# Building the retention masks on chip and reordering the first sequence of a decoder layer

## The chip, the core and the metric

The kernel runs on one NeuronCore of a Trainium2 chip. The metric is the device time of one execution in microseconds. A core has five engines with instruction queues of their own, each run in order: TensorE (PE), VectorE (DVE), ScalarE (ACT), GpSimd (POOL) and SyncE (SP), which here only issues transfers. They meet through semaphores.

## The reference

A post-norm decoder layer over 4 sequences of 256 tokens, width 256:

```
x = layernorm(x + retention(x))            # 16 heads, decay mask
x = layernorm(x + ssm(ctx_1024, gate=x))   # 256 channels x 16 states
x = layernorm(x + moe_ffn(x))              # 896 wide, LoRA experts, top 2 of 8
```

The part on masks, from the retention:

```
expn = jnp.maximum(diff, 0).astype(x.dtype)
dmask = jnp.where(diff >= 0, gamma[:, None, None] ** expn, 0.0)
scores = jnp.einsum('bhnd,bhmd->bhnm', q, k) * dmask
ret = jnp.einsum('bhnm,bhmv->bhnv', scores, v)
```

The retention output is normalised per head, times silu(x @ wg + bg), and projected with wo. The state space part projects the context, convolves it over 4 tokens, applies silu (u), makes a low-rank projection (dbl: step size, B and C rows), step sizes delta = softplus(...), and then state = state * exp(delta * A) + delta * u * B, y = sum of state * C, over 256 tokens.

## The kernel before

The four sequences form a pipeline written out by hand. `first(0)` on each engine computes retention and state space part of sequence 0; `stage(b, fb)` then interleaves those of sequence b with the feed-forward of fb = b - 1; the last stage has the feed-forward of sequence 3 alone. Every engine's order is the order of the calls in its block.

The state recurrence is cut into 16 units of 2 states x 256 tokens x 128 channels (`UNITS`). In `first`, a unit i needs `decays(i)` on ACT (L723, two exponentials), `drive(i)` on PE (L1186, four transposes of columns that ACT's `drive_columns` made, L874), `first_scan(i)` on DVE (L1794), `first_times_c(i)` on POOL (L630) and `add_states(i)` on PE (L1251, four transposes added into the bank acc). The ring has 4 tiles, `decay` has 2 and `drives` 3, so unit i waits for i - 4, i - 2 and i - 3.

Retention runs in chunks of 128 tokens. `scores(r)` (PE, L1322) for r = 0 to 3 fills the two gen banks, `decayed` (DVE, L1741) multiplies them by `dmask`, `values(r)` (PE, L1340) sums into ret. `token_keys` and `chunk_state` make the state that the first chunk hands to the second. `qdec` (128 x 2 x 128) holds the powers for the second chunk's queries, which POOL applies in `decayed_queries` (L611).

The masks: DVE doubles a row of powers of gamma for 16 heads seven times (L1618), SP stores it to DRAM with 16 copies, fetches it back skewed, 16 rows at a time, in eight transfers into `dmask` (L433), and twice into `qdec` (L437). SP issues the fetch of the first feed-forward weight W1 (L457) after these. The weights W1, W3, B1, B3 are split into a high part (a cast) and a low part (a subtraction), blocks of 128 x 448: `split_high`, `split_low`. In `first`, W1's four casts stand on DVE ahead of the first scan, W3's in the loop, the subtractions on POOL.

All matrix products of the first sequence's inputs (context IN, Q, DBL, DT, K, V, key transposes KN, GATE, KV) rotate through the two gen banks in the order `FIRST`. Six products of later sequences (`spare`) follow from unit 7 on, when the feed-forward banks are still idle. `conv` (DVE) needs xpad and cv from ACT's `conv_input`; u feeds `low_rank`, then `step_size` on PE, `softplus` on ACT, and `step_small`, `step_sum` on DVE, whose product with u is du; PE's `flip_inputs` (L1178) transposes du.

## Time and profile before

| | us |
|---|---|
| median of 3 runs | 425.17 |
| lowest, highest | 423.29, 426.05 |
| the profiled execution | 419.82 |
| its span | 418.1 |
| mean granted TensorE clock, share of full | 0.986 |

Busy over the span: PE 373.9 us (89%), weight load 320.6 (77%), DVE 298.5 (71%), POOL 214.9 (51%), ACT 188.8 (45%). These are means over the whole; the page also cuts the span into 40 slices with a tenths digit for each engine. In the timeline a row is a merged run of equal instructions: start, duration, engine and line, output and inputs by the program's names, count, and in brackets how long the engine had been idle before and what released it. An f32 product counts two matmul instructions for one in the program. Line L1081 is the helper through which nearly all matmuls go, L1801 the scan of the first sequence, L637 POOL's product with C there. Tiles that share memory carry the name of the tile: `ring` also holds the intermediate values of softplus, `yT` its logarithm, `dt_w` delta, `cv` du, `work` raw weights, `am` the C rows, `keep` the row of powers.

### The profile page before, as it was taken

The page shows a single profiled execution, that of the slowest core. Times are in us where ns is not written, and L with a number is a line of the kernel's source. Part 1 is how long each engine was busy: PE and PEld are TensorE (multiplying, and loading weights), DVE is VectorE, ACT ScalarE, POOL GpSimd, SP SyncE. Part 2 cuts the span into 40 slices and gives each one's busy share as a digit, 9 for nine tenths or more (in the row PEclk, how much of TensorE's full clock was granted, in tenths as well). Part 3 has the DMA queues.
Part 4 walks back from the last instruction along what each step waited for, and adds up shares of the span by engine and source line. Part 5 has one row for each costly group of instructions (what it writes and reads, how often), then busy time and mean ns, then how long its engine had stood idle before and what let it go on. Part 6 is the DMA issues. An engine that isn't in the chain of part 4 may idle for free.

```text
span 418.1 us, 7106 instructions
## 1 busy us (share of the span) xinstructions
PE 373.9 (89%) x2552; PEld 320.6 (77%) x2552; DVE 298.5 (71%) x616; ACT 188.8 (45%) x441; POOL 214.9 (51%) x223
## 2 busy tenths in 40 slices
PE   2959799899998999899898999899879998999993
PEld 1647589667787898778787898587779897899982
DVE  3386878677687995869869985879869986852224
ACT  2597597576322543477215434684324442321110
POOL 6057579106586974107895862018985842132030
PEclk9998979999999999999999999999999999999999
DMA  6998712230012212030113240030121200000000
GB/s 228 127 373 274 267 52 91 87 103 28 14 38 102 99 66 79 25 129 27 52 51 103 64 150 25 18 113 27 53 100 52 75 27 0 2 27 0 2 2 25
DMA packets 16979, 33.18 MB, mean 79 GB/s; under 512 B 2088, under 2 KB 5936, under 8 KB 16688
## 3 DMA queue, kind: packets, MB, share of 16 engines
q1 hardware_dynamic: 16032, 28.90, 22.6%
q10 hardware_dynamic: 912, 3.83, 2.3%
q8 instruction: 20, 0.33, 0.3%
q14 instruction: 15, 0.12, 0.1%
HBM read 29.18 MB, written 3.54 MB: 78 GB/s over the span
## 4 chain that ended last, share of the span: by engine, by line
PE 35%; DVE 11%; POOL 7%; issue 7%; ACT 4%; POOLq 0%; DVEq 0%; ACTq 0%
PE xf L1081 12%; PE a2p L1081 8%; PE gen L1081 6%; PE ret L1081 6%; PE acc L1081 3%; POOL ring L601 2%; DVE gen L1725 2%; DVE ring L1738 2%; POOL ring L591 1%; POOL work L698 1%; DVE cv L1645 1%; POOL xn_sb L622 1%; DVE gth L1717 1%; DVE work L2067 1%; ACT gen L739 1%
## 5 line engine op out<-in xcount | busy, mean ns | idle before, releaser
L1081 PE MATMUL xf<-am,wsplit 128*128 128x256 f32 x600 | 81.1, 285 | 0.0
L1081 PEld LDWEIGHTS xf<-am,wsplit 128*128 128x128 f32 x600 | 74.1, 189 | 2.0 <-issue 1.0
L591 POOL TENSOR_TENSOR ring<-cv,brow 128x512 f32<-128x512 f32 x48 | 64.7, 1356 | 4.0 <-PE acc L1081 2.7
L1081 PE MATMUL a2p<-work,wff_sb 128*128 128x256 f32 x224 | 58.5, 383 | 2.0 <-POOL work L698 1.8
L739 ACT ACTIVATE decay<-dt_w,nega 128x255 f32<-128x255 f32 x80 | 36.1, 505 | 35.5 <-DVE ring L1725 24.7
L698 POOL TENSOR_TENSOR work<-work,ratioT 128x256 f32<-128x256 f32 x28 | 21.4, 766 | 54.4 <-DVE work L1996 54.4
L995 ACT ACTIVATE fth<-xf 128x256 f32<-128x256 f32 x50 | 18.8, 376 | 65.6 <-PE xf L1081 65.6
L1081 PEld LDWEIGHTS a2p<-work,wff_sb 128*128 128x128 f32 x224 | 38.3, 189 | 7.4 <-POOL work L698 3.6
L1081 PE MATMUL xf<-x2s,wsplit 128*128 128x256 f32 x300 | 42.0, 288 | 1.5 <-ACT ratioT L1027 0.9
L601 POOL TENSOR_TENSOR ring<-ring,crow 128x512 f32<-128x512 f32 x24 | 30.8, 1281 | 21.7 <-issue 10.4
L1081 PEld LDWEIGHTS xf<-x2s,wsplit 128*128 128x128 f32 x300 | 37.3, 188 | 3.6 <-ACT ratioT L1027 1.3
L1081 PE MATMUL acc<-ident,ring 128*128 128x128 f32 x256 | 37.4, 277 | 2.6 <-POOL ring L601 2.0
L1985 DVE SCALAR_TENSOR_TENSOR fth<-fth,xf 128x256 f32<-128x256 f32 x50 | 20.6, 412 | 23.2 <-ACT fth L995 23.2
L1081 PEld LDWEIGHTS acc<-ident,ring 128*128 128x128 f32 x256 | 30.5, 142 | 7.7 <-POOL ring L601 2.8
L1725 DVE TENSOR_TENSOR_SCAN ring<-decay,ring 128x512 f32<-128x512 f32 x24 | 35.2, 1465 | 0.0
L667 POOL TENSOR_TENSOR cv<-dt_w,u 128x512 f32<-128x512 f32 x3 | 3.9, 1286 | 55.8 <-DVE dt_w L1707 55.8
L1725 DVE TENSOR_TENSOR_SCAN gen<-gen,ring 128x512 f32<-128x512 f32 x24 | 29.4, 1223 | 2.8 <-ACT gen L739 2.0
L1745 DVE TENSOR_TENSOR sc<-gen,dmask 128x512 f32<-128x512 f32 x32 | 20.6, 686 | 13.0 <-PE ret L1081 7.2
L637 POOL TENSOR_TENSOR ring<-ring,am 128x512 f32<-128x512 f32 x16 | 20.3, 1279 | 7.5 <-DVE ring L1801 7.5
L1081 PE MATMUL gen<-qm,kT 32*128 32x256 f32 x128 | 18.7, 409 | 6.1 <-DVE sc L1745 3.3
L1738 DVE TENSOR_TENSOR ring<-gen,crow 128x512 f32<-128x512 f32 x24 | 16.6, 691 | 9.8 <-POOL ring L601 8.3
L628 POOL TENSOR_TENSOR rs<-ve,mhalf 128x2 f32<-128x2 f32 x12 | 8.4, 700 | 28.8 <-DVE ve L1780 28.8
(248 smaller groups left out, 745.6 us busy)
## 6 DMA issues: line engine op xcount, KB each, us to landing
brow<-bc_dram SPq DMA_DIRECT2D x24, 256.0 KB, 3.6
crow<-bc_dram SPq DMA_DIRECT2D x24, 256.0 KB, 3.2
work<-in_wsp SPq DMA_DIRECT2D x2, 896.0 KB, 7.5
wff_sb<-in_wff SPq DMA_DIRECT2D x2, 896.0 KB, 7.7
am<-bc_dram ACTq DMA_DIRECT2D x1, 1536.0 KB, 10.3
wattn_sb<-in_wattn SPq DMA_DIRECT2D x1, 1280.0 KB, 5.6
xT_sb<-in_xT SPq DMA_DIRECT2D x4, 256.0 KB, 3.3
xn_sb<-in_x SPq DMA_DIRECT2D x4, 256.0 KB, 2.7
```

Source lines behind the costliest of these rows:

```text
L591: pool.tensor_tensor(ring[:, i % RING], du[:, j].unsqueeze(1).broadcast_to([P, UN, S]), brow[:, c % 2], ALU.mult).then_inc(sem["drive_read ...
L601: pool.tensor_tensor(unit, unit, crow[:, c % 2], ALU.mult).then_inc(sem["out_ready"], 1)
L628: pool.tensor_tensor(dst[:], src[:], mhalf[:], ALU.pow).then_inc(sem[done], 1)
L637: pool.tensor_tensor(unit, unit, first_c[:, c * UN:(c + 1) * UN], ALU.mult).then_inc(sem["out_ready"], 1)
L698: pool.tensor_tensor(xs[:, n % 4], fq[:, m % 2], ratioT[:], ALU.mult).then_inc(sem["xs_ready"], 1)
L739: act.activation(to[:, n, 1:], delta[:, j, 1:], ACT.Exp, scale=nega[:, j, s_:s_ + 1]).then_inc(sem["decay_ready"], 1)
L995: act.activation(fth[:, n % 2], xf[xf_bank(fb, X_MAIN + n)][:, 0], ACT.Tanh, scale=0.5).then_inc(sem["th_ready"], 1)
L1081: return pe.matmul(o, l, r, skip_group_check=True, **kw)
L1725: dve.tensor_tensor_scan(rate if i in BANKED else drive, rate, drive, 0.0, ALU.mult, ALU.add).then_inc(sem["state_ready"], 1)
L1738: dve.tensor_tensor(unit, decay_of(b, i) if i in BANKED else unit, crow[:, c % 2], ALU.mult).then_inc(sem["out_ready"], 1)
L1745: dve.tensor_tensor(sc[:, i % 2].rearrange("p (c a) i -> p c a i", c=2), gen[gen_at(b, g_sc(b) + i)][:].rearrange("p (c a i) -> p c a i", ...
L1985: dve.scalar_tensor_tensor(fs[:, n % 2], fth[:, n % 2], 1.0, o[:, 0], ALU.add, ALU.mult).then_inc(sem["s_ready"], 1)
```

## The change

The DRAM trip of the masks goes. POOL makes the identity first, PE transposes it into the idle bank xf[0], and DVE makes each head's mask by a scan: state = gamma * state + identity, 16 scans of 128 x 128 into `dmask`; two scans with start value 1 make `qdec`. The scans stand among DVE's instructions in groups of 6, 2, 2, 6 and 2. The attention weight comes in five fetches with semaphores of their own; the context and gamma are fetched by ACT's queue; the C rows of sequence 0 by SP's. K and the chunk state go to xf[1], V to ret, the gate to acc, instead of rotating through gen. W1's casts move to POOL. Round 0 of the scores goes ahead of the first scan, group statistics and mean go one unit earlier, W3's casts one later.

```diff
-FIRST = ("IN", "Q", "DBL", "DT", "K", "V", "KN", "GATE", "KV")
+FIRST = ("IN", "Q", "DBL", "DT", "KN")
+H_K, H_V, H_G, H_KV = range(1, 5)
...
-HIGH_DVE = {1: (1, 0), 2: (1, 1), 3: (1, 2), 4: (1, 3)}
+HIGH_DVE = {2: (1, 0), 3: (1, 1), 4: (1, 2), 5: (1, 3)}
 HIGH_ACT = {5: (3, 0), 6: (3, 1), 7: (3, 2), 8: (3, 3), 9: (2, 0), 10: (2, 1), 11: (2, 2), 12: (2, 3)}
-LOW_POOL = {0: (0, 2), 1: (0, 3), 2: (1, 0), 3: (1, 1), 4: (1, 2), 5: (1, 3),
+LOW_POOL = {0: (0, 2), 1: (0, 3), 3: (1, 0), 4: (1, 1), 5: (1, 2), 6: (1, 3),
             8: (3, 0), 9: (3, 1), 10: (3, 2), 11: (3, 3), 12: (2, 0)}
-HIGH_SEM = {0: ("dve_high", 0), 1: ("dve_high", PER_W), 2: ("act_high", PER_W), 3: ("act_high", 0)}
...
+            def attention_weight(i, name):
+                sp.dma_start(wattn_sb[:, i], wattn[:, i * 2 * H:(i + 1) * 2 * H].rearrange("p (k n) -> p k n", k=2)
+                             ).then_inc(sem[name], 16)
+            sp.dma_start(vec_sb[:], vec).then_inc(sem["w_vec"], 16)
+            sp.dma_start(wssm_sb[:], wssm).then_inc(sem["w_ssm"], 16)
+            attention_weight(0, "w_q")
+            sp.dma_start(xT_sb[:], xT[0]).then_inc(sem["x_in"], 16)
+            attention_weight(1, "w_k")
+            attention_weight(2, "w_v")
+            sp.dma_start(wdt_sb[:], wdt).then_inc(sem["w_dt"], 16)
             for name in GIVEN:
                 sp.sem_inc(sem[name], 1)
-            sp.dma_start(vec_sb[:], vec).then_inc(sem["w_vec"], 16)
-            sp.dma_start(ctx_sb[:], ctxT[0]).then_inc(sem["ctx_in"], 16)
-            sp.dma_start(wssm_sb[:], wssm).then_inc(sem["w_ssm"], 16)
-            sp.dma_start(gamma_sb[:], gamma).then_inc(sem["w_gamma"], 16)
-            sp.dma_start(wdt_sb[:], wdt).then_inc(sem["w_dt"], 16)
-            sp.dma_start(xT_sb[:], xT[0]).then_inc(sem["x_in"], 16)
-            sp.dma_start(wattn_sb[:], wattn).then_inc(sem["w_attn"], 16)
             sp.dma_start(rows_sb[:], rows.partition_broadcast(P)).then_inc(sem["w_rows"], 16)
+            attention_weight(3, "w_g")
             sp.dma_start(xn_sb[:], x[0]).then_inc(sem["xn_in"], 16)
-            sp.wait_ge(sem["pow_step"], 9)
-            sp.dma_start(pow_dram, powrow.unsqueeze(1).broadcast_to([HEADS, SKEW, 2 * P])).then_inc(sem["pow_out"], 16)
-            def masks():
-                sp.wait_ge(sem["pow_out"], 16)
-                for k in range(0, P, SKEW):
-                    sp.dma_start(dmask[k:k + SKEW],
-                                 bass.AP(tensor=pow_dram.tensor, offset=P - 1 - k,
-                                         ap=[[2 * P - 1, SKEW], [2 * P * SKEW, HEADS], [1, P]])).then_inc(sem["mask_in"], 16)
-                for t in range(2):
-                    sp.dma_start(qdec[:, t], bass.AP(tensor=pow_dram.tensor, offset=t * GH * 2 * P * SKEW + P,
-                                                     ap=[[2 * P * SKEW, GH], [2 * P, DH], [1, P]])).then_inc(sem["mask_in"], 16)
-                sp.dma_start(wroute_sb[:], wroute).then_inc(sem["w_route"], 16)
+            attention_weight(4, "w_o")
+            sp.dma_start(wroute_sb[:], wroute).then_inc(sem["w_route"], 16)
+            def first_rows():
+                need(sp, "bc_out", 0, 16)
+                for k, (s0, s1) in enumerate(((0, 2 * UN), (2 * UN, DS))):
+                    sp.dma_start(first_c[:, s0:s1], of(bc_dram, 0)[DS + s0:DS + s1].partition_broadcast(P)
+                                 ).then_inc(sem[f"c_first{k}"], 16)
...
                         if i == 1:
+                            first_rows()
                             sp.wait_ge(sem["spread_const"], 1)
                         if i == 3:
...
             for piece in range(len(FF_PIECES)):
+                if piece == 4:
+                    spare_inputs()
                 feed_forward_weights(piece)
...
+            def split_high(c):
+                if c == 0:
+                    pool.wait_ge(sem["w_raw0"], 16)
+                pool.tensor_copy(wflat[:, 0, 0, c * BLOCK:(c + 1) * BLOCK], raw_block(0, c)).then_inc(sem["pool_high"], 1)
...
             def first(b, nb):
+                need(pool, "u_ready", b, 1)
+                bias(b)
+                split_high(0)
+                split_high(1)
+                need(pool, "dt_step", b, 4)
+                split_high(2)
+                split_high(3)
                 decayed_queries(b)
-                bias(b)
                 split_low(0, 0)
                 split_low(0, 1)
                 for i in range(UNITS):
                     first_times_c(b, i)
                     if i == 6:
                         root(b, gvar, grs, "gn_step", 9, "gn_pow")
+                    if i == 7:
                         gated(b)
...
+            act.dma_start(gamma_b[:], gamma.partition_broadcast(P)).then_inc(sem["w_gamma"], 16)
+            act.dma_start(ctx_sb[:], ctxT[0]).then_inc(sem["ctx_in"], 16)
+            for t in range(2):
+                act.dma_start(gamma_c[:, t:t + 1], bass.AP(tensor=gamma.tensor, offset=t * GH, ap=[[1, GH], [0, DH], [1, 1]])
+                              ).then_inc(sem["w_decay"], 16)
...
                 g = bank(b, "IN")
                 need(act, "drive_ready", b, 0)
-                act.activation(xpad[:, :, DC - 1:], g, ACT.Copy).then_inc(sem["conv_in"], 1)
                 for j in range(2):
+                    if j == 1:
+                        act.activation(xpad[:, :, DC - 1:], g, ACT.Copy).then_inc(sem["conv_in"], 1)
                     act.activation(cv[:, j], g[:, j], ACT.Identity, bias=cbh[:, j:j + 1],
                                    scale=cwh[:, j, DC - 1:DC]).then_inc(sem["conv_in"], 1)
...
                 conv_input(b)
+                queries(b)
+                act.wait_ge(sem["dve_const"], 5)
                 conv_tanh(b)
-                queries(b)
+                masked(b, 0)
+                keys(b)
                 low_rank(b)
                 need(act, "dbl_ready", b, 1)
                 act.dma_start(of(bc_dram, b), dbl[DR:, :]).then_inc(sem["bc_out"], 16)
-                rates(b)
-                softplus(b)
-                keys(b)
                 act.wait_ge(sem["pool_const"], CONSTS)
                 act.activation(spreadw[:].rearrange("q i p -> q (i p)"), spread_raw, ACT.Copy).then_inc(sem["spread_const"], 1)
+                softplus(b)
+                rates(b)
+                masked(b, 1)
                 act.activation(le[:, 0, 0:2], mhalf[:], ACT.Exp).then_inc(sem["act_const"], 1)
-                need(act, "bc_out", b, 16)
-                for k, (s0, s1) in enumerate(((0, 2 * UN), (2 * UN, DS))):
-                    act.dma_start(first_c[:, s0:s1], of(bc_dram, b)[DS + s0:DS + s1].partition_broadcast(P)
-                                  ).then_inc(sem[f"c_first{k}"], 16)
-                act.wait_ge(sem["dve_const"], 5)
+                decays(b, 0)
                 drive_columns(b, 0)
-                decays(b, 0)
+                decays(b, 1)
+                drive_columns(b, 1)
                 gate_linear(b)
-                masked(b, 0)
-                decays(b, 1)
-                masked(b, 1)
-                drive_columns(b, 1)
                 decays(b, 2)
                 start_y(b)
                 gate_tanh(b)
...
+                pe.wait_ge(sem["pool_const"], EYE)
+                pe.transpose(xf[0][:, 0, 0:P], ident[:], ident[:]).then_inc(sem["eye_filled"], 1)
                 pe.wait_ge(sem["w_ssm"], 16)
                 context(b)
-                pe.wait_ge(sem["w_attn"], 16)
+                pe.wait_ge(sem["w_q"], 16)
                 need(pe, "x_in", b, 16)
                 project(b, "Q", wq)
+                pe.wait_ge(sem["w_k"], 16)
+                project_to(xf[1], wk).then_inc(sem["head_filled"], 1)
+                pe.wait_ge(sem["w_v"], 16)
+                values_to(ret, (0,))
                 low_rank(b)
-                rates(b)
+                values_to(ret, (1,)).then_inc(sem["head_filled"], 1)
                 pe.wait_ge(sem["w_dt"], 16)
                 step_size(b)
-                project(b, "K", wk)
-                token_values(b)
-                pe.wait_ge(sem["pool_const"], CONSTS)
                 token_keys(b)
-                project(b, "GATE", wg)
+                rates(b)
+                scores(b, 0)
+                pe.wait_ge(sem["w_g"], 16)
+                project_to(acc, wg).then_inc(sem["head_filled"], 1)
+                chunk_state(b)
                 flip_inputs(b)
+                pe.wait_ge(sem["mask_ready"], MASKS)
                 drive(b, 0)
+                need(pe, "kv_ready", b, 1)
                 drive(b, 1)
-                chunk_state(b)
                 for i in range(UNITS):
                     if i > 0 and i + 2 < UNITS:
                         drive(b, i + 2)
-                    if 1 <= i <= 4:
-                        values(b, i - 1)
                     if i < 4:
-                        scores(b, i)
+                        values(b, i)
+                        if i < 3:
+                            scores(b, i + 1)
                     if i == 0:
                         drive(b, 2)
+                    if i == 1:
                         start_y(b, None)
-                    else:
+                    if i > 0:
                         add_states(b, i - 1)
                     if i == 5:
                         group_mean(b)
                     if i == 6:
                         group_var(b)
                     if i == 9:
+                        pe.wait_ge(sem["w_o"], 16)
                         attention_out(b)
                     if i in SPARE_STEP:
...
+            def masks(h0, h1):
+                for h in range(h0, h1):
+                    dve.tensor_tensor_scan(dmask[:, h], gamma_b[:, h:h + 1].broadcast_to([P, P]), xf[0][:, 0, 0:P], 0.0,
+                                           ALU.mult, ALU.add).then_inc(sem["mask_ready"], 1)
+            def query_decays():
+                dve.wait_ge(sem["w_decay"], 32)
+                for t in range(2):
+                    dve.tensor_tensor_scan(qdec[:, t], gamma_c[:, t:t + 1].broadcast_to([P, P]), geps[:, 0, 0:1].broadcast_to([P, P]), 1.0,
+                                           ALU.mult, ALU.add).then_inc(sem["mask_ready"], 1)
+            dve.wait_ge(sem["w_gamma"], 16)
+            dve.wait_ge(sem["eye_filled"], 1)
+            masks(0, 6)
             dve.wait_ge(sem["act_const"], 1)
             dve.tensor_scalar(nega[:], nega[:], -1.0, None, ALU.mult).then_inc(dc, 1)
+            dve.wait_ge(sem["pool_const"], BLOCKED)
+            dve.tensor_reduce(parity[:], headblk[:].rearrange("p (w a d) -> p a d w", a=2, d=DH)[:, :, 0], AX.X, ALU.add
+                              ).then_inc(dc, 1)
+            masks(6, 8)
             dve.wait_ge(dc, 4)
...
                 conv(b)
-                step_small(b)
+                masks(10, HEADS)
...
                 token_values(b)
+                query_decays()
+                token_keys(b)
+                positive(b)
+                step_small(b)
                 step_sum(b)
                 need(dve, "dt_step", b, 4)
                 dve.tensor_tensor(du[:], delta[:], u[:], ALU.mult).then_inc(sem["du_ready"], 1)
-                dve.wait_ge(sem["mask_in"], MASKS)
-                token_keys(b)
-                for c in range(PER_W):
-                    split_high(0, c)
+                chunk_state(b)
+                decayed(b, 0)
+                decayed(b, 1)
                 for i in range(UNITS):
                     first_scan(b, i)
-                    if i == 0:
-                        chunk_state(b)
-                    if 1 <= i <= 4:
-                        decayed(b, 2 * i - 2)
-                        decayed(b, 2 * i - 1)
+                    if 1 <= i <= 3:
+                        decayed(b, 2 * i)
+                        decayed(b, 2 * i + 1)
+                    if i == 4:
+                        group_stats(b)
+                        gate_silu(b)
                     if i == 5:
-                        group_stats(b)
+                        group_mean(b)
                     if i == 6:
-                        group_mean(b)
                         group_var(b)
-                    if i == 4:
-                        gate_silu(b)
                     if i == 7:
                         group_scale(b)
                     if i in HIGH_DVE:
```

Three pieces of the order of instructions. DVE, from the convolution (of `cv`) to the second scan (`ring<-decay,xf`), before:

```order
L1645 SCALAR_TENSOR_TENSOR cv<-xpad,cwh,cv 128x256 x6
L1648 SCALAR_TENSOR_TENSOR u<-ring,cv 128x512
L1688 TENSOR_SCALAR dt_w<-ring 128x512
L1690 TENSOR_TENSOR dt_w<-ring,dt_w 128x512
L1810 TENSOR_REDUCE parity<-headblk 128x2
L1670 TENSOR_TENSOR vpad<-gen,rows_sb 128x8x16 x4
L1701 TENSOR_TENSOR dt_w<-dt_w,yT 128x512
L1707 TENSOR_TENSOR dt_w<-dt_w,ring 128x512
L1815 TENSOR_TENSOR cv<-dt_w,u 128x512
L1677 TENSOR_TENSOR sc<-gen,dmask 128x256
L1970 CAST wsplit<-work 128x448 x4
L1801 SCALAR_TENSOR_TENSOR ring<-decay,xf 128x512
```

and with the change:

```order
L1705 SCALAR_TENSOR_TENSOR u<-ring,cv 128x512
L1662 SCALAR_TENSOR_TENSOR dmask<-gamma_b,xf 128x128 x6
L1731 TENSOR_TENSOR vpad<-ret,rows_sb 128x8x16 x4
L1669 SCALAR_TENSOR_TENSOR qdec<-gamma_c,geps 128x128 x2
L1738 TENSOR_TENSOR sc<-gen,dmask 128x256
L1747 TENSOR_SCALAR ring<-gen,vec_sb 128x256 x2
L1753 TENSOR_SCALAR dt_w<-ring 128x512
L1755 TENSOR_TENSOR dt_w<-ring,dt_w 128x512
L1766 TENSOR_TENSOR dt_w<-dt_w,yT 128x512
L1772 TENSOR_TENSOR dt_w<-dt_w,ring 128x512
L1887 TENSOR_TENSOR cv<-dt_w,u 128x512
L1781 TENSOR_TENSOR kv<-xf,headblk 128x256
```

Eight scans for masks and two softplus parts have come in after u, the four casts have gone, and the chunk state kv stands directly behind du. PE, from Q to the flip of du (`a2p<-ident,cv`), before:

```order
L1081 MATMUL gen<-xT_sb,wattn_sb 128x256 x4
L1081 MATMUL gen<-u,wssm_sb 40x256 x2
L1081 MATMUL a2p<-wssm_sb,u 128x16 x4
L1081 MATMUL gen<-dbl,wdt_sb 128x256 x2
L1081 MATMUL gen<-xT_sb,wattn_sb 128x256 x4
L1081 MATMUL gen<-wattn_sb,xT_sb 128x256 x4
L1221 MATMUL gen<-ident,kT 128x128 x2
L1081 MATMUL gen<-xT_sb,wattn_sb 128x256 x4
L1183 MATMUL a2p<-ident,cv 128x128 x4
```

and with the change:

```order
L1103 MATMUL gen<-xT_sb,wattn_sb 128x256 x4
L1103 MATMUL xf<-xT_sb,wattn_sb 128x256 x4
L1103 MATMUL ret<-wattn_sb,xT_sb 128x256 x2
L1103 MATMUL gen<-u,wssm_sb 40x256 x2
L1103 MATMUL ret<-wattn_sb,xT_sb 128x256 x2
L1103 MATMUL gen<-dbl,wdt_sb 128x256 x2
L1249 MATMUL gen<-ident,kT 128x128 x2
L1103 MATMUL a2p<-wssm_sb,u 128x16 x4
L1103 MATMUL gen<-qm,kT 128x256 x4
L1103 MATMUL acc<-xT_sb,wattn_sb 128x256 x4
L1103 MATMUL xf<-vpad,sc 128x128 x4
L1208 MATMUL a2p<-ident,cv 128x128 x4
```

K and half of V now stand ahead of the low-rank product (`gen<-u`), round 0 of the scores (`gen<-qm,kT`) and the chunk state ahead of the flip.

## Rows read from the trace of the kernel before

**Rows 1.** Stretches: length, busy us of PE, PEld, DVE, ACT, POOL, granted clock, DMA share, GB/s.

```profile
5.00:10.00 5.00, 2.16 (x5) 1.26 (x5) 3.36 (x14) 1.51 (x3) 2.94 (x17) 1.00 0.96 366
30.10:58.20 28.10, 24.48 (x180) 19.47 (x180) 21.14 (x35) 19.60 (x51) 18.79 (x17) 0.82 0.62 221
51.30:58.10 6.80, 6.28 (x22) 5.44 (x22) 4.36 (x8) 5.86 (x15) 3.52 (x4) 0.51 0.01 2
58.20:74.20 16.00, 15.87 (x98) 14.03 (x96) 13.55 (x23) 12.16 (x29) 15.97 (x14) 1.00 0.27 104
```

**Rows 2.** Timeline to 24 us: start, us, engine, line, operation, count, [idle before <-releaser].

```profile
4.64 2.07 PE L1081 MATMUL gen<-ctx_sb,wssm_sb 128*128 128x256 f32 x4 [4.64 <-DMA wssm_sb<-in_wssm]
7.38 0.60 ACT L751 ACTIVATE xpad<-gen 128x512 f32<-128x512 f32 x1 [3.99 <-DVE cbh L1624]
9.00 2.47 DVE L1645 SCALAR_TENSOR_TENSOR cv<-xpad,cwh,cv 128x256 f32<-128x256 f32 x6 [1.43 <-ACT cv L753]
9.56 3.78 PE L1081 MATMUL gen<-xT_sb,wattn_sb 128*128 128x256 f32 x8 [2.84 <-DMA wattn_sb<-in_wattn]
12.16 0.69 DVE L1648 SCALAR_TENSOR_TENSOR u<-ring,cv 128x512 f32<-128x512 f32 x1 [0.70 <-ACT ring L758]
13.27 1.35 PE L1081 MATMUL gen<-u,wssm_sb 128*40 128x256 f32 x4
20.10 0.63 ACT L799 ACTIVATE yT<-ring 128x512 f32<-128x512 f32 x1
22.60 0.69 DVE L1815 TENSOR_TENSOR cv<-dt_w,u 128x512 f32<-128x512 f32 x1
```

**Rows 3.** Timeline, POOL's wait for the masks.

```profile
23.73 0.72 POOL L617 TENSOR_TENSOR qd<-q_sb,qdec 128x256 f32<-128x256 f32 x1 [15.56 <-DMA qdec<-pow_dram]
```

**Rows 4.** Timeline up to the first scan.

```profile
24.30 1.57 ACT L882 ACTIVATE brow<-a2p,bT 128x256 f32<-128x256 f32 x4 [0.71 <-PE a2p L1183]
25.72 3.19 DVE L1970 CAST wsplit<-work 128x448 fp32r<-128x448 f32 x4 [1.77 <-DMA work<-in_wsp]
28.83 1.21 DVE L1801 TENSOR_TENSOR_SCAN ring<-decay,xf 128x512 f32<-128x512 f32 x1
```

**Rows 5.** Timeline of the attention rounds among the scans.

```profile
36.21 1.62 ACT L882 ACTIVATE crow<-a2p,bT 128x256 f32<-128x256 f32 x4
36.80 1.29 DVE L1745 TENSOR_TENSOR sc<-gen,dmask 128x512 f32<-128x512 f32 x2 [1.65 <-PE gen L1081]
38.31 1.21 DVE L1801 TENSOR_TENSOR_SCAN ring<-decay,xf 128x512 f32<-128x512 f32 x1
39.56 0.51 ACT L739 ACTIVATE decay<-dt_w,nega 128x255 f32<-128x255 f32 x1 [1.73 <-DVE ring L1801]
42.23 1.21 DVE L1801 TENSOR_TENSOR_SCAN ring<-decay,xf 128x512 f32<-128x512 f32 x1
46.73 1.21 DVE L1801 TENSOR_TENSOR_SCAN ring<-decay,a2p 128x512 f32<-128x512 f32 x1
```

**Rows 6.** Timeline, start and end of the tail.

```profile
53.98 3.62 PE L1081 MATMUL gen<-wattn_sb,sc 128*128 128x256 f32 x8
56.90 2.50 POOL L637 TENSOR_TENSOR ring<-ring,am 128x512 f32<-128x512 f32 x2
76.45 0.69 DVE L1962 TENSOR_TENSOR dt_w<-acc,yT 128x512 f32<-128x512 f32 x1 [1.74 <-PE acc L1081]
```

**Rows 7.** Timeline, sizes and prices of single operations.

```profile
7.63 0.54 POOL L580 TENSOR_SCALAR headavg<-headblk 128x128 f32<-128x128 f32 x1
16.60 1.99 PE L1081 MATMUL gen<-xT_sb,wattn_sb 128*128 128x256 f32 x8
23.52 0.43 DVE L1677 TENSOR_TENSOR sc<-gen,dmask 128x256 f32<-128x256 f32 x1 [0.23 <-DMA qdec<-pow_dram]
31.41 1.14 POOL L608 TENSOR_TENSOR wsplit<-work,wsplit 128x448 fp32r<-128x448 f32 x1
58.72 0.60 PE L1196 MATMUL a2p<-ident,crow 128*128 128x128 f32 x4
```

121 lines of the change are left out of this document (69 added, 52 removed).

## The prediction

> **What bounds the kernel now.** I read the chain of waits first. It resolves only the later batches, and there the diff moves nothing but ACT's three conv_input pieces, so the first sequence is what can move: from 0 to DVE's first addition of the state output at 76.45 us [rows 6]. Then I read the timeline by engine up to that point, and the busy times by stretch. Three parts are to be seen.
>
> First, the chain to the first scan. PE starts at 4.64. ACT then stands 3.99 us on the DVE constant cbh, since DVE queues seven power steps ahead of it; conv starts at 9.00, u ends at 12.85, the low-rank matmul runs from 13.27, the logarithm ends at 20.73, du at 23.29 [rows 2]. Between Q and the low-rank matmul PE has no gap: the whole attention weight landed only at 9.56. After du ACT makes the drive columns (24.30 to 25.87), but scan 0 starts at 28.83, because DVE has four casts of W1 in front of it: 3.19 us, after a wait of 1.77 for a transfer that SP issues behind the mask fetches [rows 4]. POOL stands 15.56 us for the same masks [rows 3].
>
> Second, the rounds of attention, in a ring with the scans: scores on PE, two decay products on DVE (1.29), values on PE, the next scores. DVE gives scan 3 and scan 4 a distance of 42.23 - 38.31 = 3.92 us, against 1.21 for a scan itself [rows 5]. All four rounds lie inside the scan loop, and scan 5 comes at 46.73.
>
> Third, the tail. POOL is busy 15.97 of 16.00 us from 58.20 to 74.20, and PE 15.87; before that, from 30.10, POOL is idle 28.10 - 18.79 = 9.3 us [rows 1]. What the tail gains is therefore what POOL's unit 8 (second of the pair at 56.90, so at 58.15) and PE's first spare projection (53.98) gain [rows 6].
>
> **The change, part by part,** as times on the same clock.
>
> Start. ACT issues ctx itself, SP drops its eight semaphore increments from the front and puts wssm second; I take context at 4.1 instead of 4.64 (bounds: no gain, and 0.9, the one issue and a half that go). The bound constants now come right behind vec, so ACT starts when context's matmuls end (2.07 us, 6.2) instead of at 7.38. cv, xpad, cv take 1.6; conv may begin after the second: 7.5 instead of 9.00. Its six steps (2.47) end at 10.0, tanh (0.65) waits for ACT's two query pieces (0.84), u ends at 11.6 instead of 12.85.
>
> Masks. Ten fetches and a store go, with 1.4 MB; 18 scans of 128x128 come to DVE. A 128x512 scan takes 1.21, a 128x256 product 0.43 and a 128x512 one 0.69 [rows 2, 5, 7]. The products give 0.26 us per 256 columns and 0.17 fixed; with the same fixed part a scan has 1.04 for 512 columns, 0.26 for 128, so about 0.43; I take 0.40. Bounds are 0.30 (a quarter) and 1.21 (no scaling). Eight stand before conv: 3.3 + 3.2 + small steps of 0.5 = 7.0, covered by ACT's 7.4. Two lie beside tanh. Six follow u: 2.4 us, to 14.0, covered by PE's half of V. Two follow V: 0.8 on DVE's path. If that cover went they would cost 4 us.
>
> PE. Behind Q (9.2, with bounds 8.1 and 10.0 from the 1.99 and the 3.78 that eight such matmuls take at full and at half speed [rows 2, 7]) come K (2.0) and half of V (1.0): 12.2, against u at 11.6. So low rank starts at 12.2 instead of 13.27 and waits for PE, 0.6 late. dbl is out at 13.6, the step-size matmul runs behind V's second half to 15.1. On ACT abs, exp, table and logarithm follow without the two positive parts (0.84), which go to DVE: the logarithm ends at 18.6 instead of 20.73. DVE's own row is V (0.88), query decays, kd (0.43), two positive parts (0.8), two small steps (1.12): 18.3, so it is just ready; du ends at 20.8 instead of 23.29. Rates, scores 0, gate and chunk state, moved ahead of the flip on PE, end at 21.4, 0.6 after du; flip ends at 22.2.
>
> First scan. ACT has made bT, qm and the table load by 21.2 and decay 0 by 22.1, columns start at 22.3 (24.30 before). From columns' start to the end of both transposes is 2.2 us. The casts of W1 (3.19) are on POOL, so nothing of DVE's is left in front but kv and round 0 (1.7 us, 20.8 to 23.2). Scan 0: 24.5 instead of 28.83, **4.3 us sooner**.
>
> Loop. Only rounds 1 to 3 are left in it, at the same 3.9 us: scan 2 at 28.3, scan 3 at 32.8, scan 4 at 36.5 (42.23 before), scan 5 at 40.4 (46.73 before) behind group statistics, silu and a cast. The group mean now stands before scan 6 and the variance before scan 7, one wait of PE less in a row: scan 7 at 44.9. Spare 0 starts at 46.8 on PE (7.2 sooner), POOL's gated product ends at 50.9 and unit 8 starts there: 7.2 sooner. So the loop adds 2.9 to the 4.3.
>
> POOL. Four casts come to it: bounds 0.38 (half of DVE's quickest pair would be less) and 1.9 (3.5 times the 0.54 of a 128x128 step); I take the 1.14 of the nearest row, the 128x448 subtraction [rows 7]. Two run behind the bias before 16, two wait for delta at 20.1, with qd (0.72) and two subtractions they end at 25.6, as scan 0 does at 25.7. At 1.9 it is 1.5 us later, inside the 9.3 idle.
>
> Transfers. The first C rows now wait on SP, not on ACT, and W3 stands behind them; bc is stored from 14 on, when the 3.3 MB ahead of it have moved at the 366 GB/s of the stretch from 5 to 10 us [rows 1], so by about 12. They have until 25.7. Spare inputs wait for attention's end (37.7) ahead of A2 and W2: spare 0 comes at 46.8 and the weights after 70. ACT's conv order in later batches is worth nothing: DVE is there behind the normalisation. All nil.
>
> **The sum** is 7.2; I take 0.6 off for a dozen semaphore hops of about 0.05 that my round times leave out: **6.6 us**. The profiled execution goes from 419.82 (span 418.1 and 1.7 around it) to 413.2. It lies 5.35 under the median of the runs, 425.17, so the same saving gives **418.6**. Own range: saving 4.6 to 8.6, so 416.6 to 420.6.
>
> **Rivals.**
>
> *ACT holds the early loop.* Its columns, decays and the rest run without a gap from 24.30 to 37.83 [rows 4, 5]. From decay 0 at 21.2 to columns 3 they sum to 13.3 us, so to 34.5: 3.3 sooner only. For it: every unit needs ACT. Against: behind that point ACT stands 1.73 us for scan 3 [rows 5]. If it stays the bound: 425.2 - 3.3 = 421.9.
>
> *PE's clock.* The granted clock is 0.51 from 51.3 to 58.1, its lower level of 1.2 GHz [rows 1]; a spare projection of eight matmuls takes 3.62 there, eight at full speed 1.99 [rows 6, 7]. What stood before the fall were transposes, small matmuls and gaps. Attention now ends some nine us earlier and spare 0 only seven, so more of that thin stretch comes: three units more whose drive and sum (0.60 each [rows 7]) double, up to 3.6 us, of which I count 3.0 as not hidden. Saving 3.6: 421.6. For it: the two rows. Against: the ring of four tiles leaves sums slack.
> The Trainium skill ("TensorE: Matmul & The Clock Gate", section "Part 4: PE-mode transpose") says that transposes do not count as PE being busy in the way that lifts the clock; by that rule the fall comes right after the last attention round, and the time would be 421.6. By the rows alone I hold the low stretch to be as long as before, 418.6. By that rule the trace agrees: the fall lies in a stretch of transposes.
>
> *The mask scans do not scale.* If a scan of 128 columns cost as much as one of 512, 1.21, then conv waits 6.1 more, tanh's cover fails by 1.6, u's row grows by 4.9 and the query decays by 1.6: 14.2 us, scan 0 at 38.7, and with 2.9 from the loop the kernel is 7.0 slower: 432.2. Of the 0.81 extra per scan 14.2 / 0.81 = 17.5 scans count, so it turns at 0.40 + 6.6 / 17.5 = 0.78 us per scan. For it: no short scan is in the trace. Against: products scale nearly with columns.
>
> *More than forecast:* the idle 28 to 30 us of PE goes, and with it an early half-clock stretch; saving 9 to 11, 415.2.
>
> **Chances.** Forecast 0.62, ACT 0.12, clock 0.13, scans 0.05, more 0.08. 1% is 4.25 us, about what a measurement of this kernel can tell from none. Of the forecast 0.57 lies beyond it, 0.05 within; of ACT and clock 0.06 beyond (half their rounds hidden), 0.19 within; more is all beyond; of the scans 0.04 slower, 0.01 within. Faster 0.71, same 0.25, slower 0.04. Range for eight in ten: 414.8 to 422.3, which holds the forecast, both middle rivals and most of "more"; the scans stay out.
>
> **What would show it.** Right: u ends near 11.6, du near 20.8, scan 0 near 24.5, three distances of some 4 us and then none, spare 0 near 46.8, POOL full from about 51. A mask scan near 0.40 and a POOL cast near 1.1. Wrong: low rank waiting for PE by more than 1 us; DVE's masks still running when xpad is there; a half-clock stretch that begins before 45; scan 0 early but scan 5 less than 5 us sooner, which would be ACT; or a tail where POOL or PE shows gaps, so that the gain is given back.

## The result, and the profile after

The changed kernel takes 420.82 us (median of 16 runs, 418.61 to 423.94), the kernel before beside it 425.18 (16 runs, 422.21 to 426.32). The ratio is 0.9924, with an interval of 0.9902 to 0.9945: 3.2 us less. The forecast, 418.6, is a ratio of 0.9845 and 6.6 us less. The direction was right and the range for eight in ten (414.8 to 422.3) holds the time; the forecast's own range (416.6 to 420.6) just misses it, and the size was twice too large. By the prediction's own line of 1%, 3.2 us count as the same, to which it gave 0.25. The ratios here and below leave out executions that took over 1.5% more than the quickest of their kernel.

The profiled execution of after took 422.0 us (span 420.2), that of before 419.82. Set against their medians, before's was 5.4 us short and after's 1.2 long, so the two spans say nothing of the change. I compare places in the first sequence, and for times the ratios. Before's profile is also an unusual one: of 68 executions of that kernel timed beside the experiments none was quicker than 420.19, and their granted clock has a median of 0.978 where the profiled one has 0.986. After's profiled 0.976 is the median of its own 16. A mean of 0.986 over a span of 418 with half the speed in the low part makes some 12 us at the lower clock; by the same estimate before usually spends some 19, and after some 20. A low stretch that stands in after's profile and not in before's can therefore be a difference of executions.

These rows answer to those shown of before. The stretches, with the columns of [rows 1]:

```profile
5.00:10.00 5.00, 3.78 (x8) 2.68 (x9) 2.87 (x11) 1.63 (x4) 2.48 (x17) 1.00 0.66 238
21.00:27.60 6.60, 6.60 (x22) 5.14 (x23) 2.77 (x4) 4.44 (x9) 3.73 (x5) 0.50 1.01 386
48.30:55.00 6.70, 5.87 (x23) 4.71 (x23) 4.94 (x8) 4.84 (x12) 6.42 (x6) 0.50 0.76 304
58.20:74.20 16.00, 14.96 (x88) 13.17 (x88) 13.38 (x23) 12.82 (x31) 15.68 (x14) 1.00 0.28 111
```

Two things stand out. From 5 to 10 us only 238 GB/s move, where before moved 366. And the granted clock is 0.50, its lower level, in two stretches of some 6.6 us. Before's profile has one such late [rows 1] and a shorter one from 31 to 34.4, inside the loop; it has none ahead of scan 0.

The timeline of after up to the first scan (columns of [rows 2]):

```profile
3.83 1.97 DVE L1662 TENSOR_TENSOR_SCAN dmask<-gamma_b,xf 128x128 f32<-128x128 f32 x6
5.38 2.05 PE L1103 MATMUL gen<-ctx_sb,wssm_sb 128*128 128x256 f32 x4 [3.06 <-DMA ctx_sb<-in_ctxT]
8.26 3.75 PE L1103 MATMUL gen<-xT_sb,wattn_sb 128*128 128x256 f32 x8 [0.83 <-DMA xT_sb<-in_xT]
11.80 3.04 PE L1103 MATMUL xf<-xT_sb,wattn_sb 128*128 128x256 f32 x8
13.44 0.69 DVE L1705 SCALAR_TENSOR_TENSOR u<-ring,cv 128x512 f32<-128x512 f32 x1 [1.61 <-ACT ring L781]
15.63 1.06 PE L1103 MATMUL gen<-u,wssm_sb 128*40 128x256 f32 x4
16.84 1.06 POOL L610 CAST wsplit<-work 128x448 fp32r<-128x448 f32 x2 [1.30 <-DMA work<-in_wsp]
22.93 3.78 PE L1103 MATMUL acc<-xT_sb,wattn_sb 128*128 128x256 f32 x8
23.84 0.69 DVE L1887 TENSOR_TENSOR cv<-dt_w,u 128x512 f32<-128x512 f32 x1
26.50 1.66 PE L1103 MATMUL xf<-vpad,sc 128*128 128x128 f32 x8
28.00 0.60 PE L1208 MATMUL a2p<-ident,cv 128*128 128x128 f32 x4
28.70 1.57 ACT L908 ACTIVATE brow<-a2p,bT 128x256 f32<-128x256 f32 x4 [3.22 <-PE a2p L1208]
30.87 2.33 DVE L1870 TENSOR_TENSOR_SCAN ring<-decay,xf 128x512 f32<-128x512 f32 x2 [1.04 <-PE xf L1221]
```

Read it from its end. Scan 0 starts at 30.87, 2.0 us later than before (28.83 [rows 4]); 24.5 was forecast. Columns waited 3.22 us for the flip. The flip waited for no data: du was there at 24.53, but PE had the gate product (3.78, at half clock) and the chunk state (1.66) in front of it. Further up, the low-rank matmul starts 1.5 us after u's end (14.13), because Q took 3.75, K 3.04, and half of V stood before it. And Q itself began only at 8.26, behind 0.83 of waiting for xT.

From there on the change does as it should. The loop and the tail of after, with the end of PE's wait ahead of the second low stretch:

```profile
38.72 1.21 DVE L1870 TENSOR_TENSOR_SCAN ring<-decay,xf 128x512 f32<-128x512 f32 x1
46.88 1.21 DVE L1870 TENSOR_TENSOR_SCAN ring<-decay,a2p 128x512 f32<-128x512 f32 x1
48.14 1.06 PE L1221 MATMUL a2p<-ident,brow 128*128 128x128 f32 x4 [2.14 <-DVE ring L1870]
53.23 2.80 PE L1103 MATMUL gen<-wattn_sb,sc 128*128 128x256 f32 x8
57.86 1.26 POOL L647 TENSOR_TENSOR ring<-ring,am 128x512 f32<-128x512 f32 x1
76.17 0.69 DVE L2031 TENSOR_TENSOR dt_w<-acc,yT 128x512 f32<-128x512 f32 x1 [1.74 <-PE acc L1103]
```

Scan 3 stands at 38.72 (38.31 before) and scan 5 at 46.88 (46.73 before): the 2.0 us that scan 0 is late are caught up by the loop with its three rounds. The first addition of the state output comes at 76.17, 0.28 sooner than in before's short execution [rows 6]. I call this row the **first addition** below; it is the mark by which the experiments are read. There is one profile of each kernel. In after and in the first two experiments the code ahead of the gate is the same, and yet K takes 3.04, 1.89 and 2.03 us, so places in single profiles differ by a microsecond for no edit at all.

### The profile page after: what moved, and what is told of

Same layout as the page of the kernel before. It is cut to its first block, busy times and chain, and to the rows that moved or that the text cites. A ratio compares the mean times of both kernels' runs of the same rounds, so it can differ in the third digit from the quotient of the medians.

```text
span 420.2 us, 7116 instructions
## 1 busy us (share of the span) xinstructions
PE 379.9 (90%) x2553; PEld 326.2 (78%) x2553; DVE 301.6 (72%) x623; ACT 187.9 (45%) x439; POOL 217.1 (52%) x226
## 4 chain that ended last, share of the span: by engine, by line
PE 42%; DVE 8%; POOL 6%; issue 5%; ACT 3%; POOLq 0%; DVEq 0%; ACTq 0%
PE xf L1103 16%; PE a2p L1103 9%; PE gen L1103 7%; PE ret L1103 6%; PE acc L1103 4%; POOL ring L604 2%; DVE cv L1700 1%; POOL xn_sb L632 1%; POOL ring L594 1%; DVE ring L1807 1%; DVE work L2136 1%; DVE ring L1794 1%; POOL work L715 1%; DVE gen L1794 1%; POOL rs L638 1%
## 5 line engine op out<-in xcount | busy, mean ns | idle before, releaser
L1103 PE MATMUL xf<-am,wsplit 128*128 128x256 f32 x600 | 83.1, 289 | 0.0
L1103 PEld LDWEIGHTS xf<-am,wsplit 128*128 128x128 f32 x600 | 75.8, 190 | 1.9 <-issue 1.0
L1103 PE MATMUL acc<-ident,ring 128*128 128x128 f32 x256 | 38.7, 284 | 4.7 <-POOL ring L647 2.6
L1103 PEld LDWEIGHTS acc<-ident,ring 128*128 128x128 f32 x256 | 31.4, 146 | 10.2 <-POOL ring L647 3.7
```

The source lines that it names most:

```text
L1103: return pe.matmul(o, l, r, skip_group_check=True, **kw)
```

## Experiments

Each stands with its ratio to the kernel before, timed beside it on the same chip. Unless said otherwise each starts from the changed kernel.

### Order on PE: the gate's place

```diff
                 rates(b)
-                scores(b, 0)
                 pe.wait_ge(sem["w_g"], 16)
                 project_to(acc, wg).then_inc(sem["head_filled"], 1)
+                scores(b, 0)
                 chunk_state(b)
```

> Changed kernel, with the gate product moved one step up on PE, between the rates and round 0 of the scores, where PE stood idle for 0.9 us. Order theory (the gate stands between du and the flip): the flip no longer waits for it, flip at about 25 instead of 28.0, scan 0 at 28 instead of 30.87, time about 2.5 us under the changed kernel. Clock theory (the PE work ahead of the flip runs at half speed, wherever it stands): gate 3.8, scores 2, chunk state 1.7 in a row from 20, flip at 27.6, under 0.5 us gained, unless the closed gap keeps the clock up. Loop theory (what comes before the first scan is given back in the loop anyway): scan 0 sooner, unit 8 on POOL not, time the same.

Measured: 0.9879 (0.9839 to 0.992), 419.02 us. Its timeline:

```profile
17.56 1.97 PE L1103 MATMUL acc<-xT_sb,wattn_sb 128*128 128x256 f32 x8
22.32 0.66 PE L1208 MATMUL a2p<-ident,cv 128*128 128x128 f32 x4 [0.64 <-DVE cv L1887]
25.26 2.33 DVE L1870 TENSOR_TENSOR_SCAN ring<-decay,xf 128x512 f32<-128x512 f32 x2 [1.47 <-PE xf L1221]
70.59 0.69 DVE L2031 TENSOR_TENSOR dt_w<-acc,yT 128x512 f32<-128x512 f32 x1 [1.74 <-PE acc L1103]
```

The gate takes 1.97, the flip now waits for du and not du for the flip, and scan 0 is 5.6 us sooner than in after. The first addition is 5.6 sooner too: what the head gains, loop and tail pass on. The time follows by some 2 us only, and its interval overlaps that of the change (0.9902 to 0.9945). That execution's Q and K were also quicker (2.52 and 1.89), which the edit did not touch; its u came 1.1 us sooner by that. So this run alone does not part order from clock.

The other direction, the gate behind the first two drives:

```diff
                 scores(b, 0)
-                pe.wait_ge(sem["w_g"], 16)
-                project_to(acc, wg).then_inc(sem["head_filled"], 1)
                 chunk_state(b)
...
                 drive(b, 1)
+                pe.wait_ge(sem["w_g"], 16)
+                project_to(acc, wg).then_inc(sem["head_filled"], 1)
```

> Changed kernel, with the gate product moved behind the drives of units 0 and 1 on PE. Order theory: flip at about 25, scan 0 at 27.5 to 28, round 1 later by the gate's 2 to 3.8 us, so scan 2 only 1 to 1.5 us sooner; time 1 to 1.5 us under the changed kernel. Clock theory: PE stands still for ACT's columns and the gate is at half speed behind them; scan 2 no sooner, time within 0.5 us. Loop theory: scan 0 three us sooner and the time the same.

Measured: 0.9943 (0.9914 to 0.9972). The flip comes at 23.75 and scan 0 at 26.94, 3.9 us sooner than in after, but the gate now stands at 27.48 ahead of the first round's values, and scan 2 comes at 33.58, 6.6 behind scan 0. First addition 75.26. The gain of 1 to 1.5 us that was expected did not come. So not every place behind du is good: in this one the loop gives it back.

### Clock: matmuls whose result nobody reads

```diff
                 pe.transpose(xf[0][:, 0, 0:P], ident[:], ident[:]).then_inc(sem["eye_filled"], 1)
+                filler(7)
                 pe.wait_ge(sem["w_ssm"], 16)
                 context(b)
+                filler(2)
...
+            def filler(n):
+                for _ in range(n):
+                    mm(a2p[0][:, 0, 0:P], ident[:], ident[:], start=True, stop=True)
```

> Changed kernel, with nine extra 128x128 matmuls of the identity into an idle bank, seven ahead of the context product and two behind it; their results are not used. Clock theory: the granted clock is up when Q and K come, Q 2.0 instead of 3.75 and K 2.0 instead of 3.04, low rank at 14.2 or sooner instead of 15.63, du 1.5 sooner, time 1.5 to 2.5 us under the changed kernel. Order theory: Q and K are quicker but the gate still stands ahead of the flip; at most 1.5 us. Transfer theory (Q waits for xT until 8.3): fillers end before, Q starts no sooner; the gain is only its duration.

Measured: 0.9868 (0.9826 to 0.991), 418.88 us.

```profile
8.38 1.97 PE L1103 MATMUL gen<-xT_sb,wattn_sb 128*128 128x256 f32 x8 [1.26 <-DMA xT_sb<-in_xT]
19.21 3.68 PE L1103 MATMUL acc<-xT_sb,wattn_sb 128*128 128x256 f32 x8
26.48 2.33 DVE L1877 TENSOR_TENSOR_SCAN ring<-decay,xf 128x512 f32<-128x512 f32 x2 [1.04 <-PE xf L1226]
```

Q starts no sooner (8.38) but takes 1.97 instead of 3.75. Scan 0 is 4.4 us sooner with the old place of the gate, though the gate still falls into a low stretch (3.68). So the slow start of PE costs something by itself: some 2.4 us by the ratios, with intervals that just overlap.

Both edits together:

> Both edits of the two kernels before: gate product ahead of round 0, and nine fillers in the head. Clock theory: PE never falls to half speed before the flip, flip right behind du, scan 0 near 26, time 4 to 5 us under the changed kernel, more than the two alone. Order theory: the sum of the two, 3 to 4 us. Loop theory: nothing.

Measured: 0.9871 (0.9826 to 0.9917), no more than either, where 3 to 5 us under the change were expected. The flip comes at 21.77 and scan 0 at 24.71, but then the scores of round 1 take 2.08 (twice 1.13): the low stretch moved into the loop, scan 2 comes at 30.46. First addition 72.75, later than with the gate's move alone.

The same fillers in the kernel before:

```diff
+                pe.wait_ge(sem["pool_const"], 6)
+                filler(7)
                 pe.wait_ge(sem["w_ssm"], 16)
                 context(b)
+                filler(2)
                 pe.wait_ge(sem["w_attn"], 16)
```

> The kernel before with 7 matmuls of 128 columns ahead of context and 2 behind it, results unused, on a tile that is idle then. Clock theory: the lower clock costs the changed kernel more than the kernel before, because the changed one has K, V, scores, gate and chunk state on PE ahead of the flip, and the kernel before hides its head's PE work behind the weight's landing (9.56) and behind softplus. So here Q falls from 3.78 to about 2.0, the low-rank matmul starts at u (12.9) instead of 13.27, and DVE's first addition comes 0.4 us sooner at most: ratio 0.998 to 1. Rival (the lower clock is worth the same 2 us in both kernels, so it is no reason for the miss): du 1.5 us sooner, ratio 0.995.

Measured: 1.0007 (0.9959 to 1.0055). Six of its twelve executions, which the ratio leaves out, took 427.8 to 429.4 us, longer than any of the 23 of the kernel before beside them (426.68 at most), so there is no gain here and perhaps a loss. Q takes 1.99 and the low-rank matmul stays at 13.31, as expected: in the old order little on PE stood between u and du. By these two runs the half-speed start costs the changed order, which put K and half of V ahead of the low-rank matmul, and not the old one.

### Parts of the change alone, in the kernel before

W1's casts on POOL behind the bias (the second place) instead of on DVE ahead of scan 0:

```diff
-                for c in range(PER_W):
-                    split_high(0, c)
...
+                for c in range(PER_W):
+                    split_high(c)
```

> The kernel before with one part of the change alone: W1's four casts stand on POOL behind the bias, not on DVE ahead of scan 0. In the kernel before scan 0 starts at 28.83 behind 1.77 us of waiting for the transfer and 3.19 us of casts, and the drive columns end at 25.87. If the loop passes on what its first scan gains: scan 0 near 26.5, DVE's first addition of the state output about 2.3 us sooner (74.2), ratio to before 0.9945. If the loop gives it back (ACT's columns and decays without a gap hold the early rounds): scan 0 near 26.5, scan 5 less than 1 us sooner, ratio 0.999.

Measured: 1.0013 (0.9971 to 1.0055), no difference (one of its twelve executions, at 941 us, is left out).

```profile
25.93 2.07 POOL L607 CAST wsplit<-work 128x448 fp32r<-128x448 f32 x4
27.10 1.22 DVE L1810 TENSOR_TENSOR_SCAN ring<-decay,xf 128x512 f32<-128x512 f32 x1 [2.86 <-ACT decay L747]
40.63 1.22 DVE L1810 TENSOR_TENSOR_SCAN ring<-decay,xf 128x512 f32<-128x512 f32 x1
33.00:41.50 8.50, 8.23 (x46) 6.12 (x48) 3.27 (x5) 5.23 (x14) 4.30 (x4) 0.50 0.82 262
```

Scan 0 waits for ACT and starts 1.7 us sooner. Then a low stretch (last row, columns of [rows 1]) holds the rounds, and scan 3 comes at 40.63, 2.3 later than before's. Before's own profile has a shorter one there, from 31 to 34.4; whether its usual execution looks like this one I can't say, since one profile each is all there is.

The masks alone, made by scans, with the old order, casts and weight fetch (the power row, its store and the ten fetches go, the three gamma fetches of the change come):

```diff
-            masks()
...
+            masks(0, 6)
...
+            masks(6, 8)
...
+                if b == 0:
+                    masks(8, 10)
...
+                masks(10, HEADS)
...
                 token_values(b)
+                query_decays()
```

> The kernel before with the masks alone made by scans (16 on DVE where the change has them, 2 for the query decays behind V); no mask fetches, the old order on PE, the old fetch of the attention weight, the casts on DVE. By the reasons of the prediction: xpad does not stand for cbh, u at 11.8; but Q still waits for the whole weight, so the low-rank matmul stays at 13.3 at half clock and du at 23; the casts need not wait for their transfer, so scan 0 comes near 27.1 instead of 28.83, and the first addition 1.7 us sooner, ratio 0.996. If fetches of masks were also what slows the weight's landing, Q starts before 9 and all comes a further 0.5 to 1 us sooner, ratio 0.994. If the small gamma fetches slow the start as they seem to in the changed kernel: context 0.7 us later than 4.64, Q still bound by the weight.

Measured: 1.0145 (1.0095 to 1.0194): slower, where 0.996 was expected.

```profile
12.63 3.50 PE L1066 MATMUL gen<-xT_sb,wattn_sb 128*128 128x256 f32 x8 [4.82 <-DMA wattn_sb<-in_wattn]
13.32 1.97 DVE L1604 TENSOR_TENSOR_SCAN dmask<-gamma_b,xf 128x128 f32<-128x128 f32 x6
31.12 1.21 DVE L1796 TENSOR_TENSOR_SCAN ring<-decay,xf 128x512 f32<-128x512 f32 x1
```

The scans cost what they should (six in 1.97). But the attention weight lands at 12.6 instead of 9.56, and two things are new beside it: two small gamma fetches ahead of it, and W1's 896 KB, issued at 5.8 instead of 17.2 because no mask fetch holds it back. From 2 to 4 us, before W1 is issued, only 43 GB/s move where before moved 154, so the small fetches have a part in it. What W1's early fetch costs was not run by itself.

With the weight in five pieces, Q's first, each waited for where it is used:

```diff
-            sp.dma_start(wattn_sb[:], wattn).then_inc(sem["w_attn"], 16)
+            for i, name in enumerate(("w_q", "w_k", "w_v", "w_g", "w_o")):
+                sp.dma_start(wattn_sb[:, i], wattn[:, i * 2 * H:(i + 1) * 2 * H].rearrange("p (k n) -> p k n", k=2)
+                             ).then_inc(sem[name], 16)
```

> The kernel before with the masks made by scans (that alone was 1.45% slower, with Q waiting for the whole weight until 12.63 instead of 9.56) and the attention weight fetched in five pieces, Q's first, each waited for where it is used. If the whole weight's later landing was what made the masks alone slower: Q starts near 8.5, the low-rank matmul near 13, du near 23, first addition back at 76 to 77 instead of 84.7, ratio 0.995 to 1.0. If it was something else (16 scans on DVE ahead of u and V, the query decays behind V): Q at 8.5 and the first addition still beyond 80, ratio 1.008 or more.

Measured: 1.0061 (1.0031 to 1.0091), Q at 9.70, first addition 78.75. The first addition lies between the two forecasts. The pieces give back 0.8% of the 1.45. And with the two gamma-by-head fetches issued behind conv_input as well (the edit stands with the transfers below):

> The kernel before with scanned masks and the attention weight in five pieces (1.006 by itself, context 5.76, Q 9.70), with the two gamma-by-head fetches issued behind conv_input. If the small descriptors cost the same there: context near 4.9, Q near 8, u 11.7 instead of 12.74, low rank 1.3 us sooner, du 23; ratio 1.002 to 1.004, so still no gain: what is left is the old order (query decays and 16 scans on DVE's path behind V, casts ahead of scan 0), which the change moves. If they cost nothing there: as before, 1.006.

Measured: 1.011 (1.0046 to 1.0173), where 1.002 to 1.004 was expected: not a gain over the last, though its head starts sooner.

```profile
6.83 2.99 PE L1068 MATMUL gen<-xT_sb,wattn_sb 128*128 128x256 f32 x8 [0.20 <-DMA wattn_sb<-in_wattn]
18.01 3.78 PE L1068 MATMUL gen<-xT_sb,wattn_sb 128*128 128x256 f32 x8
26.65 1.71 POOL L605 TENSOR_TENSOR xn_sb<-xn_sb,rows_sb 128x512 f32<-128x512 f32 x1
27.27 1.64 DVE L1818 TENSOR_TENSOR cv<-dt_w,u 128x512 f32<-128x512 f32 x1
30.00:42.00 12.00, 10.60 (x52) 8.09 (x52) 7.84 (x9) 12.00 (x32) 8.51 (x8) 0.50 0.30 97
```

Q starts 2.9 us sooner and u comes at 11.52, but K falls into a low stretch (3.78), V's product (2.36) partly too, du comes at 27.27, and the clock is low again from 30 to 42. PE had stood idle for 2.5 us ahead of the low-rank matmul, which was there at 12.36; that sooner data made gaps and the gaps the half-speed matmuls is my reading, and no run filled them here. One more cost of the masks alone shows in all three of these kernels: du's product takes 1.64 where it takes 0.69 in before [rows 2]. In before POOL does its query decays and bias behind du, since they wait for the mask fetches (23.73 [rows 3]); here they come sooner, and the bias runs beside du's product.

### Transfers: the two gamma-by-head fetches, and ctx

```diff
-            act.dma_start(gamma_b[:], gamma.partition_broadcast(P)).then_inc(sem["w_gamma"], 16)
             act.dma_start(ctx_sb[:], ctxT[0]).then_inc(sem["ctx_in"], 16)
-            for t in range(2):
-                act.dma_start(gamma_c[:, t:t + 1], bass.AP(tensor=gamma.tensor, offset=t * GH, ap=[[1, GH], [0, DH], [1, 1]])
-                              ).then_inc(sem["w_decay"], 16)
+            act.dma_start(gamma_b[:], gamma.partition_broadcast(P)).then_inc(sem["w_gamma"], 16)
...
                 conv_input(b)
+                for t in range(2):
+                    act.dma_start(gamma_c[:, t:t + 1], bass.AP(tensor=gamma.tensor, offset=t * GH, ap=[[1, GH], [0, DH], [1, 1]])
+                                  ).then_inc(sem["w_decay"], 16)
```

First together with the gate's move:

> The change with the gate product ahead of the first scores (as in the first experiment), and the head's small fetches moved: ctx is ACT's first issue, gamma by rows the second, and the two fetches of gamma by head (512 values of 4 bytes each) go out behind conv_input. Transfer theory: the small descriptors hold the queues, so context starts near 4.6 instead of 5.8 (its time in the first experiment), conv and u 1 us sooner (11.4), Q still waits for xT (8.3, or 7.5 if the small ones were ahead of it too); first addition near 69.7, ratio 0.986. Rival (landing is set by the bytes asked for, not by the small ones): context at 5.3 or later, u at 12.3, ratio 0.988 as in the first experiment.

(Each fetch by head has 128 values of 4 bytes, 0.5 KB, not 512 values.)

Measured: 0.9874 (0.9817 to 0.9931). Context comes at 4.73 and Q at 6.84, without a wait; u at 11.87 and scan 0 at 25.11, then a low stretch at 24 to 28, first addition 71.51. Then the same edit with the gate left where the change has it:

> The change as it is, with nothing but the fetches moved: ctx is ACT's first issue, gamma by rows the second, gamma by head goes out behind conv_input. It separates the transfers' share of the miss from the order's. With the gate first that move brought context from 5.8 to 4.7 and u from 12.35 to 11.9. Transfer theory: here context comes near 4.7 (5.35 in the change), Q at 6.9 (8.26), K, half of V and the low-rank matmul 1.3 sooner (14.3 instead of 15.6), du at 23, the flip still behind the gate; first addition 1 to 1.5 us sooner than 76.2, ratio to before 0.989. Order theory alone: the gate's place decides, so u and low rank earlier but the flip not by more than 0.5, ratio 0.992.

Measured: 0.9834 (0.979 to 0.9878), 416.89 us, close to the ratio that the prediction had for the change (0.9845) and more than was expected here (0.989). Nor did the gate's move add to it: with both the ratio was 0.9874.

```profile
4.67 2.08 PE L1103 MATMUL gen<-ctx_sb,wssm_sb 128*128 128x256 f32 x4 [2.35 <-DMA wssm_sb<-in_wssm]
6.99 2.85 PE L1103 MATMUL gen<-xT_sb,wattn_sb 128*128 128x256 f32 x8 [0.25 <-DMA xT_sb<-in_xT]
12.37 1.06 PE L1103 MATMUL gen<-u,wssm_sb 128*40 128x256 f32 x4
20.58 0.69 DVE L1887 TENSOR_TENSOR cv<-dt_w,u 128x512 f32<-128x512 f32 x1
23.18 0.60 PE L1208 MATMUL a2p<-ident,cv 128*128 128x128 f32 x4
26.05 2.33 DVE L1870 TENSOR_TENSOR_SCAN ring<-decay,xf 128x512 f32<-128x512 f32 x2 [1.05 <-PE xf L1221]
71.37 0.69 DVE L2031 TENSOR_TENSOR dt_w<-acc,yT 128x512 f32<-128x512 f32 x1 [1.74 <-PE acc L1103]
```

Here the prediction's points in the head are nearly met: u ends at 11.97 (11.6 forecast), the low-rank matmul starts at 12.37 (12.2), du ends at 21.27 (20.8). Scan 0 is not (26.05 against 24.5): the gate takes 3.56 in a low stretch, and the flip stands 1.9 us behind du. The two edits apart, gamma by head late, and ctx first:

> The change with the two gamma-by-head fetches alone issued behind conv_input instead of in the head; gamma by rows stays ACT's first issue, ctx its second. If the small descriptors are what holds the first transfers: context near 4.9 (5.35 in the change, 4.67 with both moves), Q near 7 instead of 8.26, first addition near 72, ratio 0.984. If ctx's place is the reason: context at 5.3, Q at 8 or later, ratio 0.992 as the change.

> The change with ctx alone moved to ACT's first issue; gamma by rows second, the two gamma-by-head fetches third and fourth in the head as in the change. If the small descriptors are the reason: context starts with wssm as before, 5.2, Q at 8, ratio 0.991. If ctx's place is: context near 4.7, Q still bound by xT (7.5 to 8.3), ratio 0.986.

Measured: 0.9848 (0.9803 to 0.9894) for gamma by head late, 0.9861 (0.9799 to 0.9924) for ctx first. The first interval lies wholly below the change's, the second does not, but the two ratios can't be told from each other: it is the rows that part the two edits. The profiled execution of the second took 422.39, its median is 419.43, so I read only its start. Gamma late, then ctx first:

```profile
5.46 2.05 PE L1103 MATMUL gen<-ctx_sb,wssm_sb 128*128 128x256 f32 x4 [3.15 <-DMA ctx_sb<-in_ctxT]
7.30 3.12 PE L1103 MATMUL gen<-xT_sb,wattn_sb 128*128 128x256 f32 x8
26.54 2.33 DVE L1870 TENSOR_TENSOR_SCAN ring<-decay,xf 128x512 f32<-128x512 f32 x2 [1.04 <-PE xf L1221]
```

```profile
4.69 2.08 PE L1103 MATMUL gen<-ctx_sb,wssm_sb 128*128 128x256 f32 x4 [2.38 <-DMA wssm_sb<-in_wssm]
8.23 3.75 PE L1103 MATMUL gen<-xT_sb,wattn_sb 128*128 128x256 f32 x8 [1.46 <-DMA xT_sb<-in_xT]
```

The transfer of xT, in the change and with gamma late (KB, us from issue to landing):

```profile
xT_sb<-in_xT SPq DMA_DIRECT2D x1, 256.0 KB, 6.0
xT_sb<-in_xT SPq DMA_DIRECT2D x1, 256.0 KB, 4.4
```

The small fetches hold xT, not ctx: with them out of the head xT takes 4.4 us from issue to landing, with them 6.0 in the change and 5.9 with ctx first. Ctx is held by its place. Of the two only gamma late brings Q forward: in its profile Q starts 1.0 us sooner, without a gap before it, and takes 3.12, K takes 1.89, and scan 0 comes 4.3 us sooner. K was as quick in the first experiment without this edit, so not all of the 4.3 is the transfers'.

### The fastest version

The fetches moved, the gate first, and fillers on the idle V bank:

```diff
                 chunk_state(b)
+                filler(ret[:, 0, 0:P], 3)
                 flip_inputs(b)
+                filler(ret[:, 0, 0:P], 6)
```

> The change with the gate product first and the small fetches moved (as in the experiment on the fetch order), and with 3 + 6 matmuls of 128 columns, results unused, ahead of and behind the flip, where PE stands idle (1.26 busy us of 3 from 21 to 24 there) before the granted clock falls to 0.50 at 24. Clock theory: the fall follows that gap; without it the first rounds run at full clock, scans 1 to 3 come 4 us apart, scan 5 at 40.5 instead of 42.2, first addition near 69.5 instead of 71.5. Rival (the fall comes from the thin matmuls of the front themselves and only moves): a low stretch of some 3 us at another place before 36, first addition at 71 or later, ratio 0.987 or worse.

Measured: 0.9806 (0.9775 to 0.9837), 416.4 us, the fastest of all. Against the change's 0.9924 it is 0.988, some 5 us less. Against the fetches moved alone (0.9834) the intervals overlap.

```profile
24.51 2.33 DVE L1877 TENSOR_TENSOR_SCAN ring<-decay,xf 128x512 f32<-128x512 f32 x2 [1.47 <-PE xf L1226]
30.00:42.00 12.00, 9.51 (x94) 7.72 (x91) 10.23 (x18) 7.00 (x19) 6.98 (x6) 1.00 0.84 276
46.88 2.02 PE L1103 MATMUL gen<-wattn_sb,sc 128*128 128x256 f32 x8
69.18 0.69 DVE L2038 TENSOR_TENSOR dt_w<-acc,yT 128x512 f32<-128x512 f32 x1 [2.33 <-PE acc L1103]
```

The clock is not low before 43.7, and then only to 47.1; scan 0 at 24.51, scan 5 at 40.52 and the first spare projection at 46.88: the prediction for the change had 24.5, 40.4 and 46.8. Twelve more fillers ahead of the two group-mean products:

```diff
                 gen_free(b, g_sc(b) + G_MEAN)
+                if b == 0:
+                    filler(gen[gen_at(b, g_sc(b) + G_MEAN)][:, 0:P], 6)
                 need(pe, "gn_step", b, 5)
```

> As the kernel with matmuls ahead of and behind the flip, and with 6 more ahead of each of the two group-mean products, where PE stands 2.1 us for DVE and 1.2 for POOL before the low stretch of 43 to 51. Clock theory: that stretch goes too, the first spare projection takes 2.0 instead of 3.15, POOL's unit 8 comes 1 us sooner, first addition near 68.5, ratio 0.983. Rival (the stretch is hidden behind ACT's and POOL's units, or the extra matmuls only stand in the way): no gain over the kernel without the twelve.

Measured: 0.9852 (0.9807 to 0.9898), no gain over the kernel without them. The low stretch near 45 goes and comes back at 53 to 56; first addition 70.78.

## Why the prediction was right in direction and wrong in size

- **Start, and PE behind it: the step that failed.** I put context at 4.1, with no gain (4.64) as the worst bound, and Q's end at 9.2. It was 5.38 and 12.0. The diff adds two fetches of gamma by head to ACT's queue, behind gamma by rows and ctx and ahead of the table load, and I gave them no cost; the transfer paragraph looked only at what comes after 12 us. With them xT takes 6.0 us to land instead of 4.4, and Q starts at 8.26. Context is late for another reason: ctx stands second on ACT's queue, and where it stood first the context product started at 4.69. Moving the gamma fetches alone gave 0.9848. That this is the forecast's ratio (0.9845) is in part luck: scan 0 stood at 26.54 there, not at 24.5. PE's half speed at the start adds to the delay: I had Q's duration as a bound (3.78), but K at full speed (2.0) where it took 3.04 in this profile.
- **The flip 0.6 behind du's end, by order on PE: failed with it.** I had the gate end before du. At half clock scores, gate and chunk state took 7.5 us where full speed has 4.3 (1.13 + 1.97 + 1.16 with the gate moved), and the flip came 3.5 us after du. "A half-clock stretch that begins before 45" was named as a sign of being wrong, and it was there at 21. How the 3.4 us that are missing fall on these two steps is not shown: gamma late, fillers and the gate's move give back 3.2, 2.4 and 1.9 us, each alone, and the gate's move together with the fillers, or with the fetches moved, gave no more than the better of the two alone.
- **Mask scans: right.** Six in 1.97, 0.33 each, where I took 0.40 with a bound of 0.30. The rival in which they do not scale is out.
- **Casts on POOL: right that they are hidden.** 0.53 each, half of the 1.14 that I took. But alone they are worth nothing that the ratio shows (1.0013).
- **Loop with three rounds: right.** Scan 0 to scan 5 is 16.0 us in after and 17.9 before, where 15.9 was forecast. Up to the first spare projection the forecast gain was 2.9, and it is 2.8 (53.23 against 53.98, behind a scan 0 that is 2.0 late).
- **ACT as the bound: out.** This rival allowed 3.3 us against before's rows; the first addition is 5.9 us sooner than there with the gate first, and 7.3 in the fastest version. Where scan 0 came sooner and neither the gate nor a new low stretch stood in the loop, the first addition followed by the same amount (5.6 and 5.6 us against after with the gate first, 4.4 and 4.4 with fillers, 4.3 and 4.3 with gamma late, 4.8 and 4.8 with the fetches moved). Where one did, it did not follow (3.9 and 0.9 with the gate behind the drives, 6.2 and 3.4 with gate first and fillers).
- **The clock rival: it was half right.** I had priced the low stretch after attention. That one is as long as before (6.7 us, where [rows 1] has 6.8) and starts 3 us sooner, at 48.3; the last values had ended at 43.6. The Trainium skill ("TensorE: Matmul & The Clock Gate", section "Part 4: PE-mode transpose") says that a transpose doesn't count as PE being busy in the same way. From it the prediction had the fall right behind attention; it came 4.7 us later, and PE had stood idle for 2.14 us before it, so this trace does not tell the rule from the idle time. The stretch that cost was another, in the head.
- **What stays open.** By the first addition the change saves 0.3 us against before's profile, by the ratio 3.2. Two kernels with the old order up to the flip (casts on POOL, fillers) show it at 79.36 and 79.03 instead of 76.45, so before's profile may be short by 2.6 to 2.9 there; its clock of 0.986, above the usual 0.978, points the same way. That fits, but it is a guess from three profiles. The prediction took its rows from that profile, so its early low stretch of 3.4 us may be shorter than usual as well. Nor does the time keep all of the head's gain: with the gate moved 5.6 us at the first addition gave some 2 us. Later low stretches would do it; they weren't taken away one by one. The 0.6 us that the sum takes off for semaphore hops stands on no row shown.

## What to carry to other kernels

Before the first matmul, cost every fetch that a change adds, however few its bytes: two of half a kilobyte each, in elements of 4 bytes, held a 256 KB fetch up by 1.6 us here. Read a forecast's rows from an execution near the median, or say how far off it is. Work moved ahead on PE has to be costed at both clock levels, with the gap in front of it in view, and what hides a step at full speed may not hide it at half. Where a wait goes, look at what it kept apart: here the wait for the masks had kept W1's fetch away from the attention weight's and POOL's products away from du's.

## What the runs showed of the hardware

- Eight matmuls of 256 columns took 3.75 behind a gap at the start and 1.97 with nine unused ones ahead, while the granted clock was recorded as 1.00 in both. At the start the rows' clock does not tell the speed; the duration does.
- A scan of 128 columns on DVE takes 0.33 where one of 512 takes 1.21.
- A 128x448 cast takes 0.53 on POOL (two in 1.06), and 0.79 each (two in 1.58) where the first runs beside DVE's product du. The 128x512 product du takes 0.69 on DVE in before, and 1.64 beside POOL's product of the same size in the last kernel with scanned masks.
- A low stretch whose gap is filled or passed came at another place instead: the first one falls at 21 in the change, at 25 with gate first and fillers, at 24 with the fetches and the gate moved, and at 43.7 in the fastest version. None of the 17 profiles is free of one.
